# The start of a four-layer kernel laid out anew: loads split and reordered, mask factors moved to another engine, weight splits moved behind the first norm

## The reference

```
x = x + 0.5 * ffn0(layernorm(x))      # two layers of local attention + gelu MLP
x = x + attn(layernorm(x))            # 16 heads, scores + 0.3 * log(mask + 1e-6)
x = x + 0.5 * ffn0(layernorm(x))
x = x + 0.5 * moe(layernorm(x))
x = x + ttt(layernorm(x))             # two test-time training steps
x = x + 0.5 * moe(layernorm(x))

pos = arange(L) / L * 2 pi
pq, pk, pz = pos_q + phase[h,0], pos_k + phase[h,1], (pos_q + pos_k) / 2 + phase[h,2]
mask = sigmoid((sin(pq)cos(pk) + sin(pk)cos(pz) + sin(pz)cos(pq) - threshold) / (temperature + 1e-6))
```

## Time and profile before

| | us |
|---|---|
| median of 3 runs | 2389.69 |
| lowest and highest of them | 2375.82, 2392.6 |
| span of the profiled execution, from its first instruction to its last | 2362.6 |
| PE busy in it | 1891.8 (80%) |
| DVE, ACT, POOL busy | 1565.0, 1234.5, 1064.1 |
| first matmul of the kernel starts at | 32.12 |

### The profile page before, as it was taken

The page is one execution under the profiler, slowest core; times in us unless marked ns, Lnnn a source line. Parts: engine busy times, 40 slices in busy tenths (PEclk is TensorE's granted clock), DMA queues, the critical chain, the costliest instruction groups (busy, mean ns, idle before and its releaser), DMA issues.

```text
span 2362.6 us, 43352 instructions
## 1 busy us (share of the span) xinstructions
PE 1891.8 (80%) x14880; PEld 1192.0 (50%) x14880; DVE 1565.0 (66%) x2479; ACT 1234.5 (52%) x2820; POOL 1064.1 (45%) x838
## 2 busy tenths in 40 slices
PE   2799999759888886589999972896698898884696
PEld 1555655425555554255655641684344644632485
DVE  5687887458999896668887736684454445326486
ACT  2467666447999895467666633342522222234242
POOL 2566566136777675365666506132231033004233
PEclk9799999967999898699999975897799999996798
DMA  6000000020010011000000021204000000000202
GB/s 227 2 2 2 2 2 2 12 84 18 21 26 20 20 25 44 0 2 1 2 2 2 2 107 36 57 22 153 0 0 1 0 0 1 0 0 23 64 22 70
DMA packets 43931, 63.36 MB, mean 27 GB/s; under 512 B 7504, under 2 KB 33488, under 8 KB 42736
## 3 DMA queue, kind: packets, MB, share of 16 engines
q1 hardware_dynamic: 39232, 51.96, 7.2%
q0 software_dynamic: 4544, 9.35, 1.2%
HBM read 45.26 MB, written 21.18 MB: 28 GB/s over the span
## 4 chain that ended last, share of the span: by engine, by line
issue 29%; PE 19%; DVE 5%; ACT 4%; DMA 2%; SPq 1%; POOL 1%; DVEq 0%; POOLq 0%; ACTq 0%
PE PS L1729 3%; PE PS L1711 2%; PE PS L448 2%; ACT arena L635 1%; PE PS L1713 1%; PE PS L1712 1%; PE PS L1719 1%; DVE arena L760 1%; PE PS L482 1%; PE PS L471 1%; PE PS L500 1%; DMA arena<-sorted_x 1%; PE PS L514 1%; PE PS L507 1%; DVE arena L773 1%
## 5 line engine op out<-in xcount | busy, mean ns | idle before, releaser
L1503 POOL TENSOR_TENSOR arena<-arena 128x1024 f32<-128x1024 f32 x128 | 299.9, 2363 | 126.9 <-ACT arena L1437 126.9
L635 ACT ACTIVATE arena<-PS,arena 128x128 f32<-128x128 f32 x512 | 180.7, 371 | 118.5 <-DVE arena L787 118.1
L955 POOL TENSOR_TENSOR arena<-arena 128x512 f32<-128x512 f32 x128 | 132.6, 1041 | 223.8 <-DVE arena L794 222.0
L318 PE MATMUL PS<-arena_r 128*128 128x512 f32 x216 | 120.3, 557 | 103.6 <-DVE arena_r L1924 42.8
L1411 PE MATMUL PS<-con,arena 128*128 128x128 f32 x1024 | 154.7, 295 | 49.6 <-DVE arena L1487 48.3
L760 DVE SCALAR_TENSOR_TENSOR arena<-PS,fcol,big 128x512 f32<-128x512 f32 x256 | 177.3, 741 | 14.2 <-PE PS L320 7.5
L1487 DVE COPY arena<-PS 128x512 f32<-128x512 f32 x256 | 165.1, 683 | 20.8 <-PE PS L1411 20.8
L1411 PEld LDWEIGHTS PS<-con,arena 128*128 128x128 f32 x1024 | 116.9, 148 | 121.0 <-issue 95.4
L1437 ACT ACTIVATE arena<-PS,arena 128x512 f32<-128x512 f32 x256 | 155.1, 688 | 38.9 <-DVE arena L1468 37.3
L1448 ACT ACTIVATE arena<-arena 128x512 f32<-128x512 f32 x256 | 162.5, 636 | 23.3 <-DVE arena L1475 17.2
L2031 POOL DMA_INDIRECT expert_y<-arena x78 | 74.8, 959 | 206.0 <-DVE arena L1990 202.3
(11 more groups left out here) (366 smaller groups left out, 4807.5 us busy)
## 6 DMA issues: line engine op xcount, KB each, us to landing
big<-in_gu SPq DMA_DIRECT2D x16, 512.0 KB, 8.2
sorted_x<-in_slots SPq DMA_DIRECT2D x2, 2515.5 KB, 15.2
arena<-sorted_x SPq DMA_DIRECT2D x6, 774.0 KB, 7.2
big<-in_dn SPq DMA_DIRECT2D x16, 256.0 KB, 8.5
arena<-expert_y SPq DMA_DIRECT2D x16, 256.0 KB, 3.3
big<-in_wqkv SPq DMA_DIRECT2D x2, 1536.0 KB, 8.9
arena<-q_split SPq DMA_DIRECT2D x96, 32.0 KB
arena<-k_split SPq DMA_DIRECT2D x96, 32.0 KB
```

What stands on the lines that cost most here:

```text
L318: pe.matmul(bank, w_hi, hi, start=first, stop=False)
L635: act.activation(pr[:, u % 2, t, :], PS[:, u % 2, t * P:(t + 1) * P], ACT.Exp, bias=nmax[:, u % 2, t:t + 1], accum_out=psum_[:, u % 2, t:t ...
L955: g.tensor_tensor(pn[:, u % 2, :, :], pr[:, u % 2, :, :], pinv[:, u % 2, :].unsqueeze(2).broadcast_to([P, TPB, P]), ALU.mult).then_inc(s(" ...
L1503: g.tensor_tensor(a, a, mk[:, hp, 2 * half:2 * half + 2, :], ALU.mult).then_inc(s("a_masked"), 1)
```

## The change

- SP first loads row 0 of `xT` alone, then `phase` and `pos`, both now laid out on 128 partitions: a head has 8 partitions (CHUNKS), each with 64 (CW) of the 512 positions. These three raise `first_loads`. Then come layer 0 of `wqkv` and `con` (`con_loaded`), `fcol` and `rot` (`rot_loaded`), the rest (`ffn_loaded`), and last the constants of the attention stage. Then SP raises 83 semaphores (LATE), waits for the factors and stores them.
- POOL raises 17 semaphores (FIRST) ahead of the others that are left to it.
- DVE makes `mean_w` by a memset, runs the 12 angle instructions (now on 128 partitions) and raises `x_ready`. The conversions of `con` come behind the first centring, the attention constants behind `low(1)`.
- The building of the factors moves to POOL, behind the pads and ahead of the row sums of ffn0. The memory of the factors is now a part of `big` behind the ffn weights, no longer `arena`. [...]
- ACT squares row 0 first and copies the high weights of layer 0 after that; those of layer 1 move behind the last norm of row 0.
- The waits at the entry of ffn0 are moved to where the data is used.
- The factors are stored in DRAM in chunks, and the loads of a head in the attention stage gather 6 x 8 pieces of 64 numbers, where before they took 6 rows of 512.

```diff
+CHUNKS = P // NH
+CW = L // CHUNKS
...
+        pos = carve([4, CW])
+        m_q, m_k = carve([MF, CW]), carve([MF, CW])
+        m_t = carve([6, CW])
...
@@ ffn_pe @@
+            if f == 0:
+                pe.wait_ge(s("first_loads"), START + 48)
             ln_pe(xT[:, 0, :], e_input(f, 0), 3, 3)
+            if f == 0:
+                pe.wait_ge(s("pads_zero"), START + 6)
+                pe.wait_ge(s("consts"), START + 7)
+                pe.wait_ge(s("con_loaded"), START + 32)
...
@@ ffn_act @@
             weights = ffn_weights()
+            if f == 0:
+                ln_square(e_input(f, 0))
+                act.wait_ge(s("con_loaded"), START + 32)
             for w, hi, _ in weights[:1]:
                 act.activation(hi, w, ACT.Copy).then_inc(s("weights_high"), 1)
-            ln_act(e_input(f, 0), 3)
+            if f:
+                ln_square(e_input(f, 0))
+            ln_rstd(e_input(f, 0), 3)
+            if f == 0:
+                act.wait_ge(s("pads_zero"), START + 6)
             entered(0)
-            for w, hi, _ in weights[1:]:
-                act.activation(hi, w, ACT.Copy).then_inc(s("weights_high"), 1)
...
+            if f == 0:
+                act.wait_ge(s("ffn_loaded"), START + 80)
+                for w, hi, _ in weights[1:]:
+                    act.activation(hi, w, ACT.Copy).then_inc(s("weights_high"), 1)
             exponentials(0, 0)
...
@@ ffn_dve @@
             ln_centre(xT[:, 0, :], e_input(f, 0), 3)
+            if f == 0:
+                load_consts(v)
             low(0)
             ln_scale(e_input(f, 0), c_one, c_zero, y[:, 0, :])
...
             low(1)
+            if f == 0:
+                attn_consts(v)
             maxima(0, 0)
...
@@ ffn_zero_pads @@
-            if f == 0:
-                g.wait_ge(s("mask_stored"), START + 32)
...
@@ load_sync @@
-            sp.dma_start(phase[0:NH, :], I["phase"]).then_inc(s("phase_loaded"), 16)
-            sp.dma_start(pos[0:NH, :, :], I["pos"]).then_inc(s("phase_loaded"), 16)
-            for name, dst in (("acol", acol), ("aw", aw), ("bv_row", bv_row)):
-                sp.dma_start(dst[:], I[name]).then_inc(s("attn_loaded"), 16)
-            for name, dst in (("xT", xT[:]), ("con", con[:]), ("fcol", fcol[:]), ("wqkv", wqkv), ("rot", rot)):
-                sp.dma_start(dst, I[name]).then_inc(s("first_loads"), 16)
+            sp.dma_start(xT[:, 0, :], I["xT"][:, 0, :]).then_inc(s("first_loads"), 16)
+            sp.dma_start(phase, I["phase"]).then_inc(s("first_loads"), 16)
+            sp.dma_start(pos, I["pos"]).then_inc(s("first_loads"), 16)
+            sp.dma_start(wqkv[:, 0, :], I["wqkv"][:, 0, :]).then_inc(s("con_loaded"), 16)
+            sp.dma_start(con[:], I["con"]).then_inc(s("con_loaded"), 16)
...
+            for name in LATE:
+                sp.sem_inc(s(name), START)
+            sp.wait_ge(s("mask_rows"), START + 1)
...
@@ load_dve @@
-            mask_factors(v)
+            v.memset(mean_w[:], 1.0 / D).then_inc(s("consts"), 1)
+            mask_angles(v)
             v.wait_ge(s("columns"), START + 7)
-            v.wait_ge(s("first_loads"), START + 80)
-            v.tensor_scalar(mean_w[:], ones, 1.0 / D, None, ALU.mult).then_inc(s("consts"), 1)
+            v.tensor_copy(col[:, 7:8], c_one).then_inc(s("x_ready"), B)
...
@@ mask_factors, now on POOL (g) @@
             def angle_sum(dst, t, a, x, b, y, op):
-                then(v.tensor_scalar(t, a, x, None, ALU.mult))
-                then(v.scalar_tensor_tensor(dst, b, y, t, ALU.mult, op))
+                g.tensor_scalar(u, b, y, None, ALU.mult).then_inc(s("mask_step"), 1)
+                steps[0] += 1
+                then(g.tensor_scalar(t, a, x, None, ALU.mult))
+                then(g.tensor_tensor(dst, u, t, op))
...
@@ attn_sync, load_mask_factors @@
-                sp.dma_start(mq_st[hp][0:MF], mq_dram[bass.ds(h, 1), :, :].rearrange("a f n -> (a f) n")).then_inc(s(f"factors{hp}_loaded"), 16)
+                sp.dma_start(mq_st[hp][0:MF].rearrange("f (c n) -> f c n", c=CHUNKS), mq_dram[bass.ds(h, 1), :, :, :].rearrange("a c f n -> f (a c) n")).then_inc(s(f"factors{hp}_loaded"), 16)
...
@@ the program of POOL @@
-            for name in sorted(set(sems) - {"x_scattered", "y_scattered"}):
-                g.sem_inc(sems[name], START)
+            names = [n for n in sorted(sems) if n not in FIRST + LATE + ("x_scattered", "y_scattered")]
+            for name in FIRST + tuple(names):
+                g.sem_inc(s(name), START)
...
                     ffn_zero_pads(g, f)
+                    if f == 0:
+                        mask_factors(g)
                     ffn_pool(g, f)
```

More of the change, by code:

```diff
@@ L238, in build @@
         w2 = carve([DEPTH, 3, D])
+        pos = carve([4, CW])
+        m_q, m_k = carve([MF, CW]), carve([MF, CW])
+        m_t = carve([6, CW])
+        ang, turns, ang_f, sc, phase = (carve([8]) for _ in range(5))
+        turns_i = turns.bitcast(I32)
         stage_memory(big)
@@ L1096, in mask_factors @@
-            s0, s1, s2, c0, c1, c2 = (sc[h, i:i + 1] for i in range(6))
-            sa, ca, sh, ch = (pos[h, i, :] for i in range(4))
-            def angle_sum(dst, t, a, x, b, y, op):
-                then(v.tensor_scalar(t, a, x, None, ALU.mult))
-                then(v.scalar_tensor_tensor(dst, b, y, t, ALU.mult, op))
-            t = m_t[h, 5, :]
-            sin_q, cos_q, sin_z, cos_z, sin_k = m_q[h, 0, :], m_t[h, 1, :], m_t[h, 2, :], m_q[h, 1, :], m_t[h, 4, :]
+                then(v.tensor_scalar(ang_f[:, 0:6], ang[:, 0:6], bound, turn, op, ALU.mult))
```

143 lines of the change are left out of this document (87 added, 56 removed).

## The result

The changed kernel took 2339.38 us, the median of 4 runs (2338.21 to 2343.15). The kernel before took 2382.76 us in the same comparison, the median of 4 (2362.6 to 2392.6; the lowest is its profiled execution, for which the record has the same number as time and as span). The ratio is 0.9851, with a 95% interval of 0.9811 to 0.9891. The forecast was 2370.9 us with a range of 2358 to 2381 us. So the time lies 31.5 us under the forecast and outside the range.

The account below looks back on a forecast made before the run. The start was taken as the bound: semaphore list, DVE's factors on 16 partitions, store plus pads. 25.2 - 0.6 - 5.2 - 0.3 - 0.3 = 18.8 us: span 2362.6 to 2343.8, plus 27.1 is 2370.9 us; range 2358 to 2381.

Parts of the forecast that it names:

- The median lies 27.1 us above the span, which I keep: Whole run: 27.1 us were added to the predicted span of 2343.8 us, giving a time of 2370.9 us.
- POOL's lateness: Row 0's first sum of squares: POOL, busy with the factors, is ready 5.2 us late.
- I take 9 us: POOL ahead of the factors: a load at MODIFY_POOL_CONFIG takes 9 us, from a possible nothing to 14.8.
- The instructions: POOL's factors: 27 instructions of 64 columns take 9.2 us with their waits, plus 0.7 us for meetings with DVE.
- A tensor_scalar on POOL has no row; the nearest is the cast: POOL's factors: a tensor_scalar of 64 columns was priced like a cast, at 0.24 us.
- rival 2: POOL at row 0's sums: not late at all, load under 4 us; 24.0 us gained, 2365.7 us; chance 0.10.
- The first matmul 25.2 us earlier: Kernel start: PE's first matmul starts at 6.95 us for 32.12, a gain of 25.2 us.
- The norm 0.6 us longer: Norm of row 0: ACT's weight copy, DVE's casts and `low(0)`, and meetings with POOL add 0.6 us.
- The copy for layer 1, 0.3 us: Behind row 0's last Exp: ACT's copy for layer 1 ends after `low(1)` started before, costing 0.3 us.
- A late POOL passes on whole: Behind POOL's first sum: PE, ACT and DVE had 0.68 us or less of idleness, so the lateness passes on whole.
- The shift at 52 us is not the shift at the end: Sign against the forecast, which had all stages from the first scores at 52.3 us shifted by the same amount.
- The two other signs named there: Signs against the forecast: POOL is ready before the squares, or factor instructions are above 0.5 us each.

Follow-up runs that it names:

- the two other builds: The changed kernel built again twice with no edit, against the kernel before: 2344.18 us (ratio 0.989) and 2341.22 us (ratio 0.9866).

## Why the prediction was wrong

**The step that failed** is "The median lies 27.1 us above the span, which I keep". That surplus was taken for launch and end. Every run since that lists both has 1.8 to 1.9 us there, those of before too (2360.09 - 2358.3). The profiled execution of before, at 2362.6 us, is at the low end of its runs and not at their median. The 27.1 us were the distance between it and three longer runs, and the forecast so added 25.3 us that lie around no span. The rest of the 31.5 us is 2.5 us between the predicted and the measured span of the profiled execution and 3.8 us by which that execution was the slowest of its four. Taking the 18.8 us off the median of before's own three timed runs is the same step in other words: 2389.69 - 18.8 is 2370.9 us again. That median stood 20 us above the 2369.73 us that the kernel gives over 24 runs. With a measurement that spreads over 30 us, the range had to be laid from the lowest runs down as well as from the median.

**The term that was mis-sized** is POOL's lateness, 5.2 us predicted and 0.9 measured; it makes all of what the start gained beyond the forecast, 23.15 us at the scores where the forecast's terms add up to 19.1 (it wrote 18.5 there). It is the sum of two errors of opposite sign, and that it came out near nothing is luck: with the instructions as forecast POOL would not have been late at all.
- "I take 9 us" for MODIFY_POOL_CONFIG: 0.1 us at most. The 14.91 us of idleness in the earlier trace rows were a wait for the squares and hid nothing. The rule of the Trainium skill, GPSIMD Engine Reference, § 2.1 Instruction dispatch, of about 6 us for the first call to a freshly loaded kernel, isn't borne out by this kernel's tensor_scalar and tensor_tensor, also not at the kernel's start (0.08 us). Whether anything is freshly loaded for them no run shows.
- The instructions: 27 in 14.6 us, 11.6 for themselves where 9.2 was predicted and 3.0 beside DVE where 0.7 was put for meetings. "A tensor_scalar on POOL has no row; the nearest is the cast" was the bad proxy: 0.44 us alone for 0.24. The tensor_tensor came out at 0.32 us as worked out, copies at 0.24. One tensor_scalar beside DVE's `low(0)` took 2.02 us. This agrees with the rule of the Trainium skill, SBUF — State Buffer, § Who interferes with whom, that the prediction had weighed.

So rival 2's cause held (no load), and its consequence nearly: it had 24.0 us, and the scores show 23.15.

**What held.** The first matmul 25.2 us earlier: 24.74, since the angles waited for a load that landed 3.1 us after its issue and not 2.7; in the two other builds it landed in 2.6 and 2.5 us, and the first matmul came 25.3 and 25.4 us earlier. The norm 0.6 us longer: 0.54 measured, but not for the reason given. The copy and `low(0)`, for which the prediction had "The slack is 0.2 us", hold up nothing (7.06 us to the scaling for 7.08), with `con` in at 8.6 us where 10.1 was expected. Meetings with POOL cost some 0.2 us, and 0.36 us in front of PE's projection were not foreseen; the number held by luck. The copy for layer 1, 0.3 us: 0.16, the time from DVE's last scaling to `low(1)` being 1.38 us for 1.22. The loads in the attention stage 0.3 us: 0.2. A late POOL passes on whole: shown with 4.8 us. Together 24.74 - 0.54 - 0.88 - 0.16 give 23.16 us, and the scores show 23.15; 0.2 goes in the attention stage. The whole run at equal clock shows 25.5 ± 1.2, some 2 us more than the scores of the three builds (23.15, 23.7 and 23.8); where these come from isn't shown. "The shift at 52 us is not the shift at the end" was named as what would show the prediction wrong; it moved between 8 and 23 us on the way, where the windows show the two traces at different clocks. The two other signs named there did not come: POOL is ready behind the squares, and a factor instruction takes 0.49 us on the mean, just under the 0.5 named. With the shift fell "From there all stages are shifted by the same amount".

**The chances.** Faster by over 1% had 0.3. At equal clock the change is 1.1% with an uncertainty of about 0.05, just past the bound; the ratio first measured is 1.5%.

## What to carry to other kernels

Before a span is turned into a median, ask for a second run of the same kernel that lists both. Here the distance was 1.8 us, and by the fit the rest of the 27.1 us was the granted clock; with each run's clock beside its span, 4.7 us of 2360 become visible that medians of 12 and 24 runs hide. An early start is worth what it moves only until the next engine is late: of 1.5 us at the projection in one trace, 0.4 went in POOL and 0.9 in matmuls at the lower clock. Two builds of one program differ by 0.7 us at the first scores, so a gain of that size needs more than one trace. And work moved to an idle engine must fit between two of that engine's deadlines: the 27 instructions on POOL came 0.9 us late ahead of the first sums and 3.1 us late behind them.

## What the runs showed of the hardware

- The mean granted clock lies between 0.889 and 0.906 over 54 runs of the unchanged kernel before, on one core of three chips. Over 109 runs of all versions the span follows it by 1.73 us for 0.001, leaving 2.1 us of scatter.
- GpSimd's tensor_scalar with a scalar from memory takes 0.44 us for 128 x 64 float32, its tensor_tensor 0.32 and its copy 0.24; VectorE takes 0.25 and 0.22 for the first two. MODIFY_POOL_CONFIG ahead of them cost 0.1 us at most.
- GpSimd raises a semaphore each 0.08 us, and the order and place of 151 of them were worth 4.7 ± 1.3 us of the whole.
- A GpSimd tensor_scalar of 0.44 us took 2.02 us when it started beside a VectorE tensor_tensor of 1.80 us with both inputs in SBUF.
